# Graph attention passes on one Trainium2 core: the differences of a batch are turned behind two of the four sums of the batch in front of it, not behind all four

## The reference

```python
alpha = a_src[src] + a_dst[dst] (+ a_edge)          # one number per edge and head
alpha = leaky_relu(alpha, 0.2)
m     = segment_max(alpha, dst)                     # per receiver and head
ea    = exp(alpha - m[dst])
den   = segment_sum(ea, dst)
out   = segment_sum(xp[src] * ea[:, :, None], dst) / den
```

## Time and profile before

| | us |
|---|---|
| runs (3) | 5514.11, 5516.17 (median), 5521.95 |
| the profiled execution, its own time | 5513.13 |
| its span in the trace | 5511.1 |
| pass `g2`, first to last sum | 2941.3 to 4057 |
| pass `g3`, first to last sum | 4285.0 to 5402 |
| busy VectorE / TensorE matmul / GpSimd in the span | 4053.3 / 3842.0 / 3592.7 |

### The profile page before, as it was taken

How to read it: one execution, slowest core, us unless ns; L and a number is a source line. 1 busy time by engine, 2 the same in 40 slices (tenths; PEclk the granted TensorE clock), 3 DMA queues, 4 the chain that set the end, 5 groups by cost and what they waited for, 6 DMA issues and landing times. The chain is left out here.

```text
span 5511.1 us, 91920 instructions
## 1 busy us (share of the span) xinstructions
PE 3842.0 (70%) x21124; PEld 3006.6 (55%) x21125; DVE 4053.3 (74%) x9130; ACT 2966.4 (54%) x8412; POOL 3592.7 (65%) x3588
## 2 busy tenths in 40 slices
PE   4799999999876676666674565556564565566555
PEld 3577777777654555555553454445433455455552
DVE  4799999999873333333477788778776788888888
ACT  4799999999654545444562333333333334433442
POOL 2577777777326777777607777777712777777770
PEclk9899999999877888888896777777787777777777
DMA  8444444444214555555535555555523455555543
GB/s 267 114 98 98 99 99 98 98 99 99 75 54 123 132 135 134 134 134 133 128 136 144 144 146 146 141 146 146 144 74 94 137 145 141 142 145 144 139 137 96
DMA packets 796988, 694.06 MB, mean 126 GB/s; under 512 B 551350, under 2 KB 666903, under 8 KB 795083
## 3 DMA queue, kind: packets, MB, share of 16 engines
q0 software_dynamic: 171248, 485.46, 31.3%
q1 hardware_dynamic: 484271, 177.31, 13.5%
q10 hardware_dynamic: 141372, 30.14, 2.9%
HBM read 628.45 MB, written 64.10 MB: 126 GB/s over the span
## 5 line engine op out<-in xcount | busy, mean ns | idle before, releaser
L1189 POOL DMA_INDIRECT c0rows<-rows,c0idx x872 | 987.0, 1132 | 281.4 <-issue 267.4
L938 POOL DMA_INDIRECT g1ring<-rows,g1idx x832 | 795.6, 956 | 348.2 <-issue 248.9
L2021 POOL DMA_INDIRECT g2rows<-sender_rows,g2idx x864 | 844.4, 977 | 265.2 <-issue 262.8
L2021 POOL DMA_INDIRECT g3rows<-sender_rows,g3idx x864 | 829.3, 960 | 281.1 <-issue 259.9
L1218 ACT ACTIVATE c0z<-c0rows,c0sh 128x128 f32<-128x128 f32 x2640 | 795.4, 407 | 1.6 <-DMA c0rows<-rows,c0idx 1.6
L1076 DVE TENSOR_TENSOR acc<-acc,g1psA 128x258 f32 x660 | 279.9, 424 | 678.5 <-PE g1psA L965 522.2
L968 PE MATMUL g1psA<-g1ring,g1sel 128*128 x2640 | 461.9, 341 | 318.3 <-DMA g1ring<-rows,g1idx 216.6
L968 PEld LDWEIGHTS g1psA<-g1ring,g1sel 128*128 128x128 f32 x2640 | 441.9, 252 | 360.8 <-issue 346.1
L2055 PE MATMUL g3psA<-g3rows,g3sel 128*128 128x136 f32 x2640 | 443.4, 328 | 157.7 <-DVE g3rows L2241 102.5
L1310 PE MATMUL c0psA<-c0prod,c0sel 128*128 128x256 f32 x1760 | 546.8, 392 | 3.5 <-DVE acc L1399 3.5
L2055 PE MATMUL g2psA<-g2rows,g2sel 128*128 128x132 f32 x2640 | 435.0, 326 | 162.3 <-DVE g2rows L2241 102.4
(11 more groups left out here) (453 smaller groups left out, 8757.3 us busy)
## 6 DMA issues: line engine op xcount, KB each, us to landing
g2bc<-dst_rows SPq DMA_DIRECT2D x55, 512.0 KB, 4.0
g3bc<-dst_rows SPq DMA_DIRECT2D x55, 512.0 KB, 3.9
g1f<-in_edge_attr SPq DMA_DIRECT2D x103, 256.0 KB, 3.7
c0rows<-rows,c0idx POOLq DMA_INDIRECT x872
g2rows<-sender_rows,g2idx POOLq DMA_INDIRECT x864
g3rows<-sender_rows,g3idx POOLq DMA_INDIRECT x864
g1ring<-rows,g1idx POOLq DMA_INDIRECT x832
rbf_steps<-prep_extra POOLq DMA_DIRECT2D x7, 1024.0 KB, 11.1
```

The source lines that it names most:

```text
L938: g.indirect_dma_start(ring[:, c * U2 + u, 0:D], None, k.table, bass.IndirectOffsetOnAxis(ap=idx[b][:, u:u + 1], axis=0)).then_inc(r_sem[b ...
L1189: g.indirect_dma_start(rows[b][:, m, place(n), :], None, k.table, bass.IndirectOffsetOnAxis(ap=at[:, 4 * m + n:4 * m + n + 1], axis=0)).th ...
L2021: g.indirect_dma_start(rows[b][:, u, 0:TW], None, k.sender_rows, bass.IndirectOffsetOnAxis(ap=at[:, u:u + 1], axis=0)).then_inc(gas[b], 16)
```

## The change

Three edits in `gat`. The fourth sum gets a semaphore of its own, `q3`, and `summed` waits for the semaphore of each quarter. In TensorE's `body` the third and the fourth sum of batch t-1 move behind `factors` and `back` of batch t; they stay ahead of `spread(t+1)` and `turn(t+1)`. No arithmetic is added or taken away.

```diff
-        quarter = [(S["q0"], 1), (S["q1"], 1), (S["q2"], 1), (S["dt"], 2)]
+        quarter = [S["q0"], S["q1"], S["q2"], S["q3"]]
...
         def summed(eng, t, q):
-            signal, more = quarter[q]
-            reach(eng, signal, t + more)
+            eng.wait_ge(quarter[q], t + 1)
...
                     sums(t - 1, before, 0).then_inc(S["q0"], 1)
                     sums(t - 1, before, 1).then_inc(S["q1"], 1)
-                    sums(t - 1, before, 2).then_inc(S["q2"], 1)
-                    sums(t - 1, before, 3)
                 factors(t, b, i)
                 back(t)
+                if not first:
+                    sums(t - 1, before, 2).then_inc(S["q2"], 1)
+                    sums(t - 1, before, 3).then_inc(S["q3"], 1)
                 if not last_one:
                     spread(t + 1, at)
                     turn(t + 1)
...
-                sums(NB - 1, (NB - 1) % 3, q).then_inc(quarter[q][0], 1)
+                sums(NB - 1, (NB - 1) % 3, q).then_inc(quarter[q], 1)
```

More of the change, by code:

```diff
@@ L1918, in gat @@
     names = ["ix0", "ix1", "ix2", "ln0", "ln1", "ln2", "hd0", "hd1", "hd2", "ae0", "ae1", "ae2", "bc",
-             "init", "oh", "z", "zt", "loc", "q0", "q1", "q2", "lev", "arg", "rt", "al", "rs", "d", "dt", "w",
+             "init", "oh", "z", "zt", "loc", "q0", "q1", "q2", "q3", "lev", "arg", "rt", "al", "rs", "d", "dt", "w",
              "msg", "sel", "acc", "c", "v", "mx", "go", "sp", "be", "xb"]
```

## The result

The changed kernel takes 5735.08 us in the median of 4 runs (5733.95 to 5738.97), the kernel before 5518.38 beside it: ratio 1.0395 (95% interval 1.038 to 1.0411). It is 217 us slower; 5712 was predicted, 5600 to 5850 the range.

A forecast was written before the change was run, and what follows sets the result against it. GpSimd's gathers bound the kernel, VectorE having slack of 3.0 (g2) and 2.7 us (g3) per batch. Losses of 54 x 1.6 + 54 x 2.1 = 200 us on 5513.1 us led to 5712 us, range 5600 to 5850.

The forecast's parts named there:

- The bound: Both attention passes: GpSimd's gathers set the pace; VectorE has slack of 3.0 us (g2) and 2.7 us (g3) per batch.
- Gain of the earlier turn: `factors` and `back` come earlier, `dt` by 0.6 us; hidden behind the gathers, worth nothing or a few tenths of gather 14.
- Step 1: TensorE: third sum starts 0.46 us (g2) or 0.61 us (g3) behind the ratio; wrong if not within 0.6 us.
- Step 2: TensorE: third and fourth sum back to back from low clock, 5.77 us (g2), 5.89 us (g3); 4.14 us at full, g2.
- Step 3: VectorE: fourth add to end of `rescale`, 2.47 us in g2 and 2.43 us in g3, behind a 0.15 us semaphore.
- The sum: Loss per batch 1.6 us in g2 and 2.1 us in g3, over 54 batches each: 200 us, so 5712 us.
- Which clock: TensorE's new 4.2 us gap drops the clock to 0.50, so the third sum starts low; chance of this forecast 0.73.
- At full clock the same sum: Rival: clock stays up, VectorE's slack swallows the wait; loss 0 in g2, 0.4 us in g3; 5516 to 5540 us, chance 0.12.
- The case with the pair low to its end: Rival: third and fourth sum run wholly at low clock, 7.66 us, 205 us more, about 5917 us; chance 0.08.
- The rule weighed: Skill's rule that a burst behind a long wait is cold altogether; would make the loss twice as large.
- The waits of VectorE: Sign: VectorE waits for TensorE about 4 us before the third add, 0.3 to 2 before the fourth, in nearly all batches.
- Gathers 5 and 9 idle: Sign that the forecast is right: GpSimd stands idle at gathers 5 and 9 of a batch; no size given.

The follow-up runs named there:

- experiment 3: Changed kernel with the third sum moved back ahead of `factors` and `back`, only the fourth behind; 5518.19 us, ratio 1.0004.
- experiment 4: Kernel before with 8 unused small additions on VectorE between `rescale` and the next batch's score; 5520.35 us, ratio 1.0007.
- experiment 5: Kernel before with 16 unused small additions on VectorE between `rescale` and the next batch's score; 5586.12 us, ratio 1.0126.
- experiment 9: Changed kernel with 13 unused matmuls ahead of `factors` and without gather 9's wait for `q1`; 5522.97 us, ratio 1.0014.
- experiment 1: Changed kernel with 13 unused matmuls in TensorE's gap between the second sum and `factors`; 5522.69 us, ratio 1.0013.
- experiment 6: Kernel before with unused matmuls in TensorE's long pause, 17 between `spread` and `turn` and 5 behind `turn`; 5514.96 us, ratio 0.9995.

## Why the prediction was right, step by step

- **The bound.** Gathers full, VectorE with slack ahead of the score: borne out by experiments 3 and 4 (extra waits and extra work for nothing). Experiment 5 does not test where the slack ends, since VectorE still waited for gathers in it. That the slack in g3 is used up shows in experiments 1 and 9.
- **Gain of the earlier turn: nothing.** Borne out by experiment 9: with clock and gate out of the way the change is still at 1.0014.
- **Step 1.** Third sum 0.46 us behind the ratio in g2 and 0.61 in g3, by its first weight load. Measured 0.51 and 0.78 on average. The step took `factors` and `back` at full clock, though the forecast has it low from the start of the pair; at the low clock the stretch from the first weight load of `factors` to that of the third sum is 0.70 us in g3, not 0.51. A batch of g3 in the changed kernel:

```profile
4851.56 0.16 DVE L2218 SCALAR_TENSOR_TENSOR g3ratio<-g3al,g3quad 128x8 f32<-128x8 f32 x1
4851.85 0.50 PEld L2068 LDWEIGHTS g3psT<-g3ratio,g3hd 128*128 128x128 f32 x2 [3.82 <-issue]
...
4852.55 2.82 PEld L2054 LDWEIGHTS g3psA<-g3rows,g3sel 128*128 128x128 f32 x12
```

  By its own sign (0.6 us) step 1 was wrong in g3, by some 0.2 us.
- **Step 2, the pair.** Taken as 5.77 us in g2 and 5.89 in g3, one value for all batches. Measured from the first weight load it is 5.92 and 5.98 on average, and it varies with where the clock falls and comes back: 6.3 us in one batch shown and about a microsecond less in the next. That the average lies so near the one value taken is in part luck.
- **Step 3.** The batch shown ends `rescale` 2.6 us behind its fourth sum (3319.55 to 3322.18), as the step has it; the score starts 0.08 us before that end.
- **The sum.** A batch of 22.1 us in g2 and 22.6 in g3 was named; 22.23 and 22.80 were measured, so 1.7 us and 2.2 us lost against 1.6 and 2.1. That is 210 of the 217 us; the 54 batches were right, and steps 1 and 2 together were sized some 0.2 us too small.
- **Which clock.** The choice that decided it. At full clock the same sum gave 5516 to 5540 us; experiment 1, which is that case made, gave 5523. With the low start it gave 5712, and 5735 was measured. The case with the pair low to its end did not occur: in the second batch shown the clock is at 1.00 from 3339.3.
- **The rule weighed.** That a burst behind a long wait is cold (the Trainium skill, TensorE: Matmul & The Clock Gate, Loop structure matters more than you think, drawn there for a wait of 8 us for a DMA) holds here for the burst's beginning, behind waits of 3.3 to 6.7 us for another engine's result; for all of it, it would have cost about twice what was measured.
- **The waits of VectorE.** Ahead of the third add it stood in all 108 batches, 4.4 us in g2 and 4.8 in g3 on average, as named. Ahead of the fourth, where the sign had 0.3 to 2 us in nearly all, it stood for more than 0.1 us in 62 of them: where the clock comes back early the fourth sum hides under the third add.
- **Gathers 5 and 9 idle.** In the batch shown gather 9 stood 2.31 us for `q1`, gather 5 no more than its issue, so the half of that sign was wrong; neither sets the end, since the score did not wait for gathers.

## What to carry to other kernels

Moving work behind a wait does two things: it makes its reader wait, and it opens a gap on the engine where the work had been. The first may be hidden by slack read off the profile; the second slows the work itself if the engine is TensorE and the granted clock falls behind the gap, here by about half as much again for two sums (5.7 against 3.8 us), and that turned an even change into one of 4%. Before moving matmuls, measure the gap they leave against gaps of that length in the same trace, and look at the clock behind them. Take that as a guess and not as a rule: it held for the gaps of about 4 us here, and failed for the gap of 1.95 us in experiment 3. To find out afterwards, fill the gap with unused matmuls, and look at the clock again.

## What the runs showed that I had not expected

- The 16 matmuls of `spread` take half the time in the new place. In the kernel before their weight loads take 1.44 us, in the changed kernel 0.67 us, both at full clock:

```profile
3319.16 0.67 PEld L2037 LDWEIGHTS g2psE<-recv,g2oneT 128*128 128x128 bf16 x16
```

  They stand behind 14 matmuls of a sum there, and behind three short ones before. Each of them reads an address from a register, and the instructions for it may be worked off while the sum runs; that is an idea, not tried. Experiment 6 speaks only half for it: the 16 stand behind the same three short ones there, and take 0.69 us in the batch of g3 shown, where the fourth sum ran low, but 1.45 us in most batches of g2.
- Filling the long pause of TensorE moved the low clock to the next one (experiment 6). In this kernel the clock was not mended by filling one of the two pauses of a batch.
- A small piece of work on VectorE can lengthen GpSimd's gathers: 977 to 1006 ns on average in g2 with 16 small additions a batch (experiment 5), and that set the time, while 8 of them did not (978 ns).
